# The residual behind the output projection: added by TensorE in PSUM instead of by VectorE

## The chip, the cores and the metric

One Trainium2 chip, one of its cores. The time is the device time of one execution in microseconds (us); lower is better. A time of a kernel is the median of its executions. The five engines run side by side, each with its instructions in a fixed order, and wait for each other by semaphores: TensorE (PE in the profile, its weight loads PEld), VectorE (DVE), ScalarE (ACT), GpSimd (POOL) and SyncE (SP), which here only issues transfers.

## The reference

A decoder layer in float32 on 64 sequences of 64 tokens with 128 channels, with three residual branches:

```
x = x + attn(layernorm(x))            # 16 heads of 8, q = k = v = x Wv + bv, then Wo and bo
x = x + xattn(layernorm(x), ctx, ctx) # 16 heads of 8, softmax, no projection
x = x + ffn(layernorm(x))             # SwiGLU: one shared expert and the best of 7 experts of each token
```

The change is at the end of the first line: the sum of x and the projected attention output, and the mean and variance of that sum, from which the query of the second line is made.

## The kernel before

The 4096 tokens are 32 units (U) of 128 tokens (two sequences). The first part of the program, `phase_a`, is a software pipeline written out step by step: in step t each engine works on several units at once, and the table `LAG` says which. Unit t is normalised and transposed, unit t-1 is projected (`proj`) and its self-attention scores are computed (`S_s`), unit t-2 gets its softmax and is weighed (`soft_s`), unit t-3 gets its output projection (`out`) and the bias (`xb`), unit t-4 its query and cross-attention scores and softmax (`q`), unit t-5 to t-7 the rest of cross attention. 32 units and lags up to 7 make 39 steps; TensorE and ScalarE leave the step form after step 33 and run a tail written out by hand. Nothing schedules: each engine's `body` is its order within a step.

Then come the router, the shared expert for the 32 units, the sorting of tokens by expert, and 38 tiles of expert rows. That part is about 170 us long and is not touched.

What happens to a unit around the change, in order: VectorE divides the weighed values by the sums of the softmax (`on_s`). SyncE writes them to a buffer in device memory and reads them back in another layout (`orow`), one step later. TensorE transposes `orow` (L619), ScalarE copies the result to `onT` (L890), TensorE multiplies `onT` by the output weights into a PSUM buffer (`ps_wo`, L624). GpSimd has in the meantime added the bias to the unit's rows of x (`p_xb`, L426). At the beginning of its next step VectorE adds `ps_wo` to these rows (L1120, tile `rows_all`), takes statistics of the sum (`st_s`, L1049) and makes mean and variance (`mv`, L1060). GpSimd subtracts the mean (`xn_s`, L409), TensorE transposes `xn_s` (`query`, L597), ScalarE copies it to `qT` (L884), and TensorE computes the cross scores (L545, tile `ring,qT`).

Names in the rows: L545 with `k_s,pT` are the self-attention scores, `mx_s` and `pr_s` the maxima over them and the differences, L842 the exponentials, L554 the transposes of the exponentials, L849 their copies out of PSUM (`prT`), L566 the weighing, L855 and L576 the copy and the transpose back (`oT`). The same with x in place of s is cross attention.

TensorE's order within a step is: `query`, projection of unit t-1 (L636, L643), `oT_x` back, cross scores, transposes of `pr_s`, weighing x and s, transposes of `xn_p` and `orow`, `oT_s` back, output projection (L624), self-attention scores (L545), transposes of `pr_x` (L554).

Of the kernel before, what the change touches and what calls it, by code (L numbers as in the profile page):

```python
# [29 lines left out]
U = B // NB  # L30
# [33 lines left out]
def build(nc, x, ctxk, ctxv, wv, bv, wo, bo, rw, rb, wup, wdn, ident, hmask, tri, small, tokens, out):  # L64
    ctx = ExitStack()
    with ctx:
# [307 lines left out]
        def _(pool):  # L374
# [27 lines left out]
            def body(t, u, live):  # L402
                i = t % 2
                pool.wait_ge(sem("mv_set"), 2)
                if live("q"):
                    pool.wait_ge(sem("s_mv"), at(u["q"]))
                    if u["q"] >= 1:
                        pool.wait_ge(sem("s_qT"), u["q"])
                    nc.gpsimd.tensor_scalar(xn["s"][:], x_all[:, u["q"], :], mv[i][:, 0, 0:1], None,  # L409
                                            ALU.subtract).then_inc(sem("s_xn"), 1)  # L410
# [118 lines left out]
        def _(pe):  # L529
# [91 lines left out]
            def project(u):  # L621

                pe.wait_ge(sem("s_onT"), at(u))
                nc.tensor.matmul(ps_wo, onT[:], wo_sb[:], start=True, stop=True).then_inc(sem("s_wo"), 1)  # L624

            def body(t, u, live):
                if t == LAG["q"]:
# [201 lines left out]
        def _(act):  # L829
# [56 lines left out]
            def output(u):  # L886
# [2 lines left out]
                    act.wait_ge(sem("s_wo"), u)  # L889
                nc.scalar.copy(onT[:], ps_oT).then_inc(sem("s_onT"), 1)  # L890

            def body(t, u, live):
                if live("pv_x"):
                    turned("x", u["pv_x"], 0)
# [46 lines left out]
                    nc.scalar.copy(kx_second, zero[:, 0:1].broadcast_to([P, CHUNK * NB * HG * S])).then_inc(sem("kx_zero1"), 1)  # L941
                if live("q"):
                    exp("x", t, u["q"], 1)

            phase_a(body, last=LAST_FULL)
            step = {u: u + LAG["q"] for u in (U - 2, U - 1)}
# [6 lines left out]
            output(U - 1)  # L953
            turned_rows(2)
            exp("x", step[U - 2], U - 2, 0)
            exp("x", step[U - 2], U - 2, 1)
            turned("x", U - 2, 0)
            query(U - 1)
# [76 lines left out]
        def _(dve):  # L1035
# [7 lines left out]

            nc.vector.memset(kx[:, 0:CHUNK // 2, :, :, :], 0.0).then_inc(sem("kx_zero0"), 1)

            def moments(k, u):
                if u >= 1:
                    dve.wait_ge(sem(f"{k}_mv"), u)
                nc.vector.bn_stats(st[k][:], x_all[:, u, :]).then_inc(sem(f"{k}_st"), 1)  # L1049

            def mean_variance(k, t, u):
                dve.wait_ge(sem(f"{k}_st"), at(u))
# [53 lines left out]
            def body(t, u, live):  # L1106
                if live("st_x"):
                    dve.wait_ge(sem("x_x"), at(u["st_x"]))
                    moments("x", u["st_x"])
                if live("norm"):  # L1110
                    if u["norm"] in X_LOADS:
                        dve.wait_ge(sem(X_LOADS[u["norm"]][0]), X_LOADS[u["norm"]][1])
                    moments("p", u["norm"])
                if live("out"):
                    invert("s", u["out"])
                    normalise("s", u["out"])
                if live("q"):
                    dve.wait_ge(sem("p_xb"), at(u["q"]))
                    dve.wait_ge(sem("s_wo"), at(u["q"]))
                    nc.vector.tensor_tensor(x_all[:, u["q"], :], ps_wo, x_all[:, u["q"], :], ALU.add).then_inc(sem("s_x"), 1)  # L1120
                if live("st_x"):
                    mean_variance("x", t, u["st_x"])
                if live("q"):
                    dve.wait_ge(sem("s_x"), at(u["q"]))
                    moments("s", u["q"])
                if live("norm"):
                    mean_variance("p", t, u["norm"])
                if live("q"):
                    mean_variance("s", t, u["q"])
                if live("soft_s"):  # L1130
                    maxima("s", u["soft_s"])
                    soften("s", u["soft_s"], 0)
                    soften("s", u["soft_s"], 1)
                if live("on_x"):
                    invert("x", u["on_x"])
                    normalise("x", u["on_x"])
                if live("q"):
                    maxima("x", u["q"])
                    soften_both("x", u["q"])
                if t == 1:  # L1140
                    nc.vector.memset(kx[:, CHUNK // 2:CHUNK, :, :, :], 0.0).then_inc(sem("kx_zero0"), 1)
                    dve.wait_ge(sem("l_first"), N_FIRST)
                    dve.wait_ge(sem("l_bv"), 16)
                    link(nc.vector.tensor_reduce(dmask[:], id_sb[:].rearrange("p (h d) -> p d h", d=DK), AX.X, ALU.add))
                    link(nc.vector.tensor_tensor(bvall_sb[:].rearrange("p (h d) -> p h d", d=DK),
                                                 bvall_sb[:].rearrange("p (h d) -> p h d", d=DK),
                                                 dmask[:, :].unsqueeze(1).broadcast_to([P, H, DK]), ALU.mult))
                    link(nc.vector.tensor_reduce(bvh[:], bvall_sb[:].rearrange("p (h d) -> p h d", d=DK), AX.X, ALU.add))
                    nc.vector.tensor_copy(bvrows_sb[:].rearrange("p (b h r) -> p b h r", b=NB, h=H),
                                          bvh[:, :].unsqueeze(1).unsqueeze(3).broadcast_to([P, NB, H, S // H])).then_inc(sem("bvrows"), 1)  # L1150
                if t == 2:
                    dve.wait_ge(sem("l_second"), N_SECOND)
                    dve.wait_ge(sem("bias"), 1)
                    nc.vector.tensor_tensor(obias[:], ps_bias, bo_sb[:], ALU.add).then_inc(sem("obias"), 1)
# [197 lines left out]
```

## Time and profile before

| | |
|---|---|
| median of 3 runs | 447.25 us (446.73 to 450.13) |
| span of the profiled execution | 447.9 us |
| steps of the pipeline shown in the rows below | about 34 us to 252 us of the span |
| granted TensorE clock, whole span | 0.985 |

The profile is of one execution, and its time is the span; what lies around the span is not in the numbers, and the span lies 0.65 us above the median of the runs. Rows of the timeline give the start and the duration of an instruction, or of a run of alike instructions, merged. Durations of neighbours on one engine can overlap, since an engine begins to read for the next instruction before the last has written; the distance from start to start says how long an instruction keeps its engine.

### The profile page before, as it was taken

To read this page: it belongs to the slowest core of one execution; us is meant where nothing else is said; L and a number is where in the kernel's file an instruction comes from. 1 tells how busy PE (TensorE), PEld (TensorE's weight loads), DVE (VectorE), ACT (ScalarE), POOL (GpSimd) and SP (SyncE) were. 2 spreads that over 40 slices of the span, in tenths; PEclk is the share of its full clock that TensorE was granted. 3 is DMA by queue.
4 is the path that set the end of the run, shared out by engine and by line. 5 is a ranking of instruction groups with operands and counts; after the bars stand their busy time and mean duration, and the time that the engine had idled before them with its cause. 6 is when DMAs were issued, how large, how long until landed. Compare 5 with 4: busy or idle time off the path is not lost. (4 is left out here: it accounts for less than half of the span.)

```text
span 447.9 us, 16458 instructions
## 1 busy us (share of the span) xinstructions
PE 420.6 (94%) x5570; PEld 314.2 (70%) x5571; DVE 312.5 (70%) x767; ACT 300.6 (67%) x685; POOL 300.5 (67%) x517
## 2 busy tenths in 40 slices
PE   7889999999999999999999999999999999999990
PEld 4545655555665655555565567899998899999990
DVE  5568999989999999999999854773333444545540
ACT  7858888788888888788888865432222465666650
POOL 8547768677877868687787655278888754444442
PEclk9999999999999999999999999899999999999995
DMA  6243444444444444453433379812222355530010
GB/s 108 37 83 46 77 52 56 69 53 80 57 80 65 70 74 60 88 64 63 46 57 39 32 131 198 268 44 71 77 80 76 85 129 137 137 105 25 27 35 0
DMA packets 181088, 34.51 MB, mean 77 GB/s; under 512 B 147347, under 2 KB 178582, under 8 KB 181024
## 3 DMA queue, kind: packets, MB, share of 16 engines
q1 hardware_dynamic: 170944, 23.63, 33.2%
q0 software_dynamic: 2864, 6.36, 4.1%
q10 hardware_dynamic: 7216, 3.69, 2.9%
q8 instruction: 37, 0.61, 0.6%
q14 instruction: 27, 0.22, 0.2%
HBM read 20.13 MB, written 15.74 MB: 80 GB/s over the span
## 5 line engine op out<-in xcount | busy, mean ns | idle before, releaser
L1162 DVE TENSOR_TENSOR gT<-gT,psum 128x384 f32<-128x384 f32 x66 | 36.6, 554 | 74.2 <-PE psum L744 51.8
L975 ACT ACTIVATE gT<-psum 128x384 f32<-128x384 f32 x70 | 34.1, 487 | 49.4 <-PE psum L744 36.0
L504 POOL DMA_INDIRECT out<-yrow,token x38 | 37.0, 973 | 40.7 <-DVE yrow L1281 26.5
L443 POOL TENSOR_TENSOR k_s<-pT,hmask_sb 128x1024 f32<-128x1024 f32 x32 | 60.9, 1903 | 2.1 <-ACT pT L904 2.0
L758 PE MATMUL psum<-wdn_sb,gT 128*128 (+1 forms) x420 | 59.9, 279 | 2.0 <-DVE yrow L1281 1.0
L409 POOL TENSOR_SCALAR xn_s<-rows_all,mv 128x128 f32<-128x128 f32 x32 | 19.4, 607 | 56.6 <-DVE mv L1060 37.7
L744 PE MATMUL psum<-fhT,wtile 128*128 128x128 f32 x456 | 57.2, 275 | 0.0
L758 PEld LDWEIGHTS psum<-wdn_sb,gT 128*128 128x128 f32 x420 | 52.4, 192 | 5.0 <-issue 3.9
L744 PEld LDWEIGHTS psum<-fhT,wtile 128*128 128x128 f32 x456 | 53.9, 192 | 0.1
L744 PE MATMUL psum<-hT_all,wup_sb 128*128 (+1 forms) x384 | 49.2, 280 | 0.0
L849 ACT COPY prT_x<-psum 128x512 f32<-128x512 f32 x64 | 34.6, 589 | 20.7 <-PE psum L554 20.4
L842 ACT ACTIVATE pr_x<-pr_x,rs 128x512 f32<-128x512 f32 x64 | 45.9, 723 | 1.4 <-DVE pr_x L1077 0.5
L744 PEld LDWEIGHTS psum<-hT_all,wup_sb 128*128 128x128 f32 x384 | 46.7, 197 | 0.0
L554 PEld LDWEIGHTS psum<-id_sb,pr_s 128*128 128x128 f32 x256 | 27.3, 141 | 26.7 <-ACT pr_s L842 26.6
L554 PEld LDWEIGHTS psum<-id_sb,pr_x 128*128 128x128 f32 x256 | 27.4, 141 | 24.8 <-ACT pr_x L842 24.8
L1070 DVE TENSOR_REDUCE mx_x<-psum 128x16 f32<-128x1024 f32 x32 | 39.2, 1225 | 7.8 <-PE psum L545 7.0
L1070 DVE TENSOR_REDUCE mx_s<-psum 128x16 f32<-128x1024 f32 x32 | 39.2, 1225 | 5.4 <-PE psum L545 4.3
L1085 DVE TENSOR_TENSOR pr_s<-psum,mx_s 128x512 f32<-128x512 f32 x64 | 41.2, 686 | 1.1
L1077 DVE TENSOR_TENSOR pr_x<-psum,mx_x 128x1024 f32<-128x1024 f32 x32 | 39.2, 1225 | 2.9
L842 ACT ACTIVATE pr_s<-pr_s 128x512 f32<-128x512 f32 x64 | 38.1, 627 | 1.7 <-DVE pr_s L1085 1.7
L554 PE MATMUL psum<-id_sb,pr_s 128*128 128x128 f32 x256 | 35.5, 280 | 0.8 <-ACT pr_s L842 0.7
L849 ACT COPY prT_s<-psum 128x512 f32<-128x512 f32 x64 | 34.5, 589 | 2.2
(150 smaller groups left out, 890.0 us busy)
## 6 DMA issues: line engine op xcount, KB each, us to landing
ring<-sorted_rows SPq DMA_DIRECT2D x30, 130.0 KB
sorted_rows<-nowhere_row SPq DMA_DIRECT2D x38, 65.0 KB, 2.3
wup_sb<-in_wup SPq DMA_DIRECT2D x7, 352.0 KB, 9.6
attention_out<-on_s SPq DMA_DIRECT2D x64, 32.0 KB, 2.9
ring<-in_ctxv SPq DMA_DIRECT2D x64, 32.0 KB, 3.3
orow<-attention_out SPq DMA_DIRECT2D x32, 64.0 KB
sorted_rows<-nowhere_row SPq DMA_DIRECT2D x3, 650.0 KB, 9.1
cross_keys<-in_ctxk ACTq DMA_DIRECT2D x14, 128.0 KB, 3.1
```

The source lines that it names most:

```text
L443: nc.gpsimd.tensor_tensor(k_s[:], pT[:].rearrange("p (b k) -> p b k", b=NB).unsqueeze(2).broadcast_to([P, NB, HG, S]), hmask_sb[:, 0:HG].u ...
L504: pool.indirect_dma_start(out=out, out_offset=bass.IndirectOffsetOnAxis(ap=token[p][:, 0:1], axis=0), in_=yrow[p][:, :], in_offset=None, b ...
L554: last = nc.tensor.transpose(ps_s[k][g][:, i * P:(i + 1) * P], pr[k][:, g, 2 * i:2 * i + 2, :].rearrange("p h k -> p (h k)"), id_sb[:])
L744: last = nc.tensor.matmul(ps[p][:, c * P:(c + 1) * P], weights[:, start:start + P], tokens, start=True, stop=True)
L758: last = nc.tensor.matmul(ps_y[p], gT[p][:, c, :], wdn_sb[:, expert, c, :], start=(c == 0), stop=(c == CH - 1))
L842: nc.scalar.activation(pr[k][:, g, :, :], pr[k][:, g, :, :], ACT.Exp, scale=rs[t % 2][:, 0:1] if k == "x" else float(DK) ** -0.5).then_inc ...
L849: nc.scalar.copy(prT[k][:, g, :, :].rearrange("p i q -> p (i q)"), ps_s[k][g]).then_inc(sem(f"{k}_prT"), 1)
L975: nc.scalar.activation(gT[p][:].rearrange("p c q -> p (c q)"), ps_gate[p][:, 0:CH * P], ACT.Silu).then_inc(sem("f_act"), 1)
L1070: nc.vector.tensor_reduce(mx[k][:], both(k), AX.X, ALU.max).then_inc(sem(f"{k}_mx"), G)
L1077: nc.vector.tensor_tensor(pr[k][:], both(k), mx[k][:].unsqueeze(3).broadcast_to([P, G, HG, S]), ALU.subtract).then_inc(sem(f"{k}_sub"), G)
L1085: nc.vector.tensor_tensor(pr[k][:, g, :, :], scores_of(k, g), mx[k][:, g, :].unsqueeze(2).broadcast_to([P, HG, S]), ALU.subtract).then_inc ...
L1162: nc.vector.tensor_tensor(g, g, ps_up[p][:, 0:CH * P], ALU.mult).then_inc(sem("f_g"), 1)
```

## The change

TensorE gets a second matmul behind the output projection, into the same PSUM buffer: the identity times the unit's rows of x. The sum with the residual then stands in PSUM. VectorE's addition is gone, and its statistics read PSUM. ScalarE copies the sum back to the rows of x, at the end of its step, behind the second exponential of cross attention; in the tail this copy stands between the two exponentials of unit 30. GpSimd's subtraction of the mean waits for that copy too.

```diff
@@ gpsimd, body @@
                     pool.wait_ge(sem("s_mv"), at(u["q"]))
+                    pool.wait_ge(sem("s_x"), at(u["q"]))
@@ tensor @@
             def project(u):
 
                 pe.wait_ge(sem("s_onT"), at(u))
-                nc.tensor.matmul(ps_wo, onT[:], wo_sb[:], start=True, stop=True).then_inc(sem("s_wo"), 1)
+                nc.tensor.matmul(ps_wo, onT[:], wo_sb[:], start=True, stop=False)
+                pe.wait_ge(sem("p_xb"), at(u))
+                nc.tensor.matmul(ps_wo, id_sb[:], x_all[:, u, :], start=False, stop=True).then_inc(sem("s_wo"), 1)
@@ scalar @@
+            def residual(u):
+                act.wait_ge(sem("s_wo"), at(u))
+                act.wait_ge(sem("s_st"), at(u))
+                nc.scalar.copy(x_all[:, u, :], ps_wo).then_inc(sem("s_x"), 1)
+
...
                 if live("q"):
                     exp("x", t, u["q"], 1)
+                if live("out"):
+                    residual(u["out"])
...
             exp("x", step[U - 2], U - 2, 0)
+            residual(U - 1)
             exp("x", step[U - 2], U - 2, 1)
@@ vector, body @@
-                if live("q"):
-                    dve.wait_ge(sem("p_xb"), at(u["q"]))
-                    dve.wait_ge(sem("s_wo"), at(u["q"]))
-                    nc.vector.tensor_tensor(x_all[:, u["q"], :], ps_wo, x_all[:, u["q"], :], ALU.add).then_inc(sem("s_x"), 1)
                 if live("st_x"):
                     mean_variance("x", t, u["st_x"])
                 if live("q"):
-                    dve.wait_ge(sem("s_x"), at(u["q"]))
-                    moments("s", u["q"])
+                    dve.wait_ge(sem("s_wo"), at(u["q"]))
+                    moments("s", u["q"], ps_wo)
```

TensorE in a step of the full pipeline, from the transpose back of self attention to the transposes of cross attention. Before:

```order
L576 MATMUL psum<-id_sb,oT_s 128x128 [waits s_oe]
L576 MATMUL psum<-id_sb,oT_s 128x128
L624 MATMUL psum<-wo_sb,onT 128x128 [waits s_onT]
L545 MATMUL psum<-k_s,pT 64x512 [waits s_prT,s_khd]
L545 MATMUL psum<-k_s,pT 64x512 x3
L554 MATMUL psum<-id_sb,pr_x 128x128 [waits x_exp]
```

After:

```order
L577 MATMUL psum<-id_sb,oT_s 128x128 [waits s_oe]
L577 MATMUL psum<-id_sb,oT_s 128x128
L625 MATMUL psum<-wo_sb,onT 128x128 [waits s_onT]
L627 MATMUL psum<-rows_all,id_sb 128x128 [waits p_xb]
L546 MATMUL psum<-k_s,pT 64x512 [waits s_prT,s_khd]
L546 MATMUL psum<-k_s,pT 64x512 x3
L555 MATMUL psum<-id_sb,pr_x 128x128 [waits x_exp]
```

One matmul has come in ahead of the self-attention scores. (The profile counts a float32 matmul of this kind as two, a transpose as one.)

VectorE at the beginning of a step, up to the maxima of self attention. Before:

```order
L1101 TENSOR_TENSOR on_s<-psum,rden_s 128x128 [waits s_out,s_rden]
L1120 TENSOR_TENSOR rows_all<-psum,rows_all 128x128 [waits s_wo,p_xb]
L1060 BN_AGGR mv<-st_x 128x2 [waits px_ve,px_mean,mv_set,x_st]
L1049 BN_STATS st_s<-rows_all 128x6 [waits s_mv,s_x]
L1060 BN_AGGR mv<-st_p 128x2 [waits px_ve,px_mean,mv_set,p_st]
L1060 BN_AGGR mv<-st_s 128x2 [waits s_ve,s_xn,mv_set,s_st]
L1070 TENSOR_REDUCE mx_s<-psum 128x16 [waits s_sc]
```

After:

```order
L1112 TENSOR_TENSOR on_s<-psum,rden_s 128x128 [waits s_out,s_rden]
L1071 BN_AGGR mv<-st_x 128x2 [waits px_ve,px_mean,mv_set,x_st]
L1060 BN_STATS st_s<-psum 128x6 [waits s_mv,s_wo]
L1071 BN_AGGR mv<-st_p 128x2 [waits px_ve,px_mean,mv_set,p_st]
L1071 BN_AGGR mv<-st_s 128x2 [waits s_ve,s_xn,mv_set,s_st]
L1081 TENSOR_REDUCE mx_s<-psum 128x16 [waits s_sc]
```

The addition is gone, and the statistics wait for the matmul (`s_wo`) where they waited for the addition (`s_x`).

ScalarE at the end of a step and the beginning of the next. Before:

```order
L842 ACTIVATE pr_x<-pr_x,rs 128x512 [waits s_rs,x_sub]
L849 COPY prT_x<-psum 128x512 [waits x_pv,x_turn] x2
L884 COPY qT<-psum 128x128 [waits x_sc,s_qT]
L904 ACTIVATE pT<-psum,bv_sb 128x128 [waits s_khd,s_sc,p_pv,p_p]
L842 ACTIVATE pr_s<-pr_s 128x512 [waits s_sub] x2
```

After:

```order
L845 ACTIVATE pr_x<-pr_x,rs 128x512 [waits s_rs,x_sub]
L898 COPY rows_all<-psum 128x128 [waits s_st,s_wo]
L852 COPY prT_x<-psum 128x512 [waits x_pv,x_turn] x2
L887 COPY qT<-psum 128x128 [waits x_sc,s_qT]
L912 ACTIVATE pT<-psum,bv_sb 128x128 [waits s_khd,s_sc,p_pv,p_p]
L845 ACTIVATE pr_s<-pr_s 128x512 [waits s_sub] x2
```

A copy has come in between the last exponential and the copies of the transposed cross-attention weights.

## Rows read from the trace of the kernel before

**Rows 1.** Busy time by stretch: us, PE, PEld, DVE, ACT, POOL, granted clock, DMA.

```profile
60.00:240.00 180.00, 176.14 (x2979) 105.94 (x2975) 165.58 (x370) 152.44 (x372) 138.26 (x254) 1.00 0.45 65
```

**Rows 2.** VectorE's maxima from 31 to 259 us: durations in ns, first and last start.

```profile
L1070 DVE TENSOR_REDUCE mx_s<-psum x29: 1223/1225/1226, 34.1 to 251.7; 128x16 f32<-128x1024 f32 x29
```

**Rows 3.** Who waited for whom, 60 to 240 us: us in total, times, longest.

```profile
POOL xn_s L409 <- DVE mv L1060: 30.7, 20, 1.9
...
DVE mx_x L1070 <- PE psum L545: 3.7, 16, 0.3
...
PEld psum L619 <- DMA orow<-attention_out: 1.9, 7, 0.5
...
DVE mv L1060 <- issue: 1.2, 4, 0.4
```

**Rows 4.** Timeline of a step: start us, us, engine, line, operation.

```profile
211.76 1.09 PE L545 MATMUL psum<-k_s,pT 64*64 64x512 f32 x8
...
212.12 0.72 ACT L842 ACTIVATE pr_x<-pr_x,rs 128x512 f32<-128x512 f32 x1
...
212.77 0.18 DVE L1060 BATCH_NORM_AGGREGATE mv<-st_s 128x2 f32<-128x6 f32 x1
...
212.99 1.23 DVE L1070 TENSOR_REDUCE mx_s<-psum 128x16 f32<-128x1024 f32 x1
213.12 0.61 POOL L409 TENSOR_SCALAR xn_s<-rows_all,mv 128x128 f32<-128x128 f32 x1 [1.41 <-DVE mv L1060]
213.47 1.07 ACT L849 COPY prT_x<-psum 128x512 f32<-128x512 f32 x2 [0.63 <-PE psum L554]
...
213.78 0.33 PE L597 MATMUL psum<-id_sb,xn_s 128*128 128x128 f32 x1
...
214.20 0.41 POOL L426 TENSOR_TENSOR rows_all<-rows_all,obias 128x128 f32<-128x128 f32 x1
...
214.25 1.29 DVE L1085 TENSOR_TENSOR pr_s<-psum,mx_s 128x512 f32<-128x512 f32 x2
...
215.02 1.18 ACT L842 ACTIVATE pr_s<-pr_s 128x512 f32<-128x512 f32 x2
...
217.18 0.59 ACT L849 COPY prT_s<-psum 128x512 f32<-128x512 f32 x1
...
218.75 0.44 PE L576 MATMUL psum<-id_sb,oT_s 128*128 128x128 f32 x2
...
219.02 0.44 PE L624 MATMUL psum<-wo_sb,onT 128*128 128x128 f32 x2
...
219.39 1.09 PE L545 MATMUL psum<-k_s,pT 64*64 64x512 f32 x8
219.51 0.29 DVE L1101 TENSOR_TENSOR on_s<-psum,rden_s 128x128 f32<-128x128 f32 x1
219.61 0.25 ACT L933 COPY xnT<-psum 128x128 f32<-128x128 f32 x1
219.72 0.28 DVE L1120 TENSOR_TENSOR rows_all<-psum,rows_all 128x128 f32<-128x128 f32 x1
...
219.92 0.17 DVE L1060 BATCH_NORM_AGGREGATE mv<-st_x 128x2 f32<-128x6 f32 x1
```

**Rows 5.** Timeline of TensorE in the expert part: passes back to back.

```profile
400.59 0.83 PE L758 MATMUL psum<-wdn_sb,gT 128*128 x6
401.26 0.27 PE L801 MATMUL psum<-id_sb,fx 128*128 128x128 f32 x1
```

**Rows 6.** Timeline of the tail: last projection, and the exponentials behind it.

```profile
263.91 0.14 PEld L619 LDWEIGHTS psum<-id_sb,orow 128*128 128x128 f32 x1 [0.31 <-DMA orow<-attention_out]
...
264.91 1.35 ACT L842 ACTIVATE pr_x<-pr_x,rs 128x512 f32<-128x512 f32 x2
```

**Rows 7.** Timeline of VectorE: the maxima at the two ends of the shortest period.

```profile
34.10 1.23 DVE L1070 TENSOR_REDUCE mx_s<-psum 128x16 f32<-128x1024 f32 x1
...
41.68 1.22 DVE L1070 TENSOR_REDUCE mx_s<-psum 128x16 f32<-128x1024 f32 x1
```

More of the change, by code:

```diff
@@ L1044, in _, with moments @@
             nc.vector.memset(kx[:, 0:CHUNK // 2, :, :, :], 0.0).then_inc(sem("kx_zero0"), 1)
-            def moments(k, u):
+            def moments(k, u, rows):
                 if u >= 1:
                     dve.wait_ge(sem(f"{k}_mv"), u)
-                nc.vector.bn_stats(st[k][:], x_all[:, u, :]).then_inc(sem(f"{k}_st"), 1)
+                nc.vector.bn_stats(st[k][:], rows).then_inc(sem(f"{k}_st"), 1)
             def mean_variance(k, t, u):
@@ L1108, in body @@
                     dve.wait_ge(sem("x_x"), at(u["st_x"]))
-                    moments("x", u["st_x"])
+                    moments("x", u["st_x"], x_all[:, u["st_x"], :])
                 if live("norm"):
@@ L1112, in body @@
                         dve.wait_ge(sem(X_LOADS[u["norm"]][0]), X_LOADS[u["norm"]][1])
-                    moments("p", u["norm"])
+                    moments("p", u["norm"], x_all[:, u["norm"], :])
                 if live("out"):
```

## The prediction

> **What bounds the kernel now.** I read the busy times by stretch first, then the timeline of one step, then the waits. In the pipeline's full steps VectorE is busy 165.58 of 180 us (92%) and TensorE 176.14 (98%) [rows 1]. Neither figure decides: TensorE's rows overlap, and VectorE's do too. So I looked for the round that closes on itself in each step. The maxima `mx_s` come 29 times between 34.1 and 251.7 us: 28 periods of 7.77 us on average [rows 2].
>
> The timeline shows the round [rows 4]. `mx_s` starts at 212.99, the differences `pr_s` at 214.25, their exponentials on ScalarE at 215.02, the second copy `prT_s` at 217.18; TensorE weighs, ScalarE copies `oT_s`, TensorE transposes it back at 218.75, runs the output projection at 219.02 and the scores of self attention at 219.39. These last 1.09, and the maxima follow 0.14 us behind their end (211.76 + 1.09 = 212.85, then 212.99). From 212.99 to 219.39 are 6.40 us, plus 1.09 and 0.14 makes 7.63. That is also the distance of the two scores in these rows (211.76 to 219.39): nothing in this round has slack, and the step lasts as long as the round. The output projection, where the change puts its matmul, is in it. VectorE's addition is not: it starts at 219.72, after the scores have started.
>
> Two things lengthen some steps from 7.63 to the mean of 7.77. `orow` comes back late from memory in 7 steps of 60 to 240 us, 1.9 us in total; and VectorE now and then loses some 0.3 us ahead of `mv` with nothing to wait for (1.2 us in 4) [rows 3], which looks like instructions being fetched.
>
> A second round runs through the query: `mv` at 212.77, `xn_s` on GpSimd 213.12 to 213.73, TensorE's query at 213.78 [rows 4]. TensorE arrives there at about the same time from the transposes before, so this round is nearly as long, but it also contains the projection and scores, through TensorE's order.
>
> **The added matmul.** It is a float32 matmul of 128 columns, as L624 is, two passes. What a pass costs in a chain: six passes of L758 take 400.59 to 401.26, 0.67 us, so 0.11 each, with different weights each time [rows 5]. The other end is L624 itself in the step, 0.37 us from its start to the scores for two passes [rows 4]; but that holds one start behind a wait for `onT` and one switch to the tiles of 64 of the scores, and both are there already. The new passes stand between the two, their weights are the identity, and their wait for `p_xb` is long over (GpSimd adds the bias at 214.20, five us earlier). I take 0.11 each, 0.22 us a step, and keep 0.37 a step as the upper end. All of it lies ahead of the scores, so all of it is in the round: 7.63 becomes 7.85.
>
> **The addition taken from VectorE.** It keeps VectorE from 219.72 to 219.92, 0.20 us a step [rows 4]. The maxima behind it wait for the scores, which are later now; so the gain becomes a wait of VectorE ahead of `mx_s`. Statistics from PSUM: the only rows of this shape that read PSUM are the addition itself (0.28) and `on_s` (0.29); I take no difference, and up to 0.1 us would be hidden in the same wait.
>
> **The copy on ScalarE.** A PSUM copy of this shape takes 0.25 (`xnT`) [rows 4]. ScalarE ends its second exponential at 212.84 and starts the next copy at 213.47, having waited 0.63 for TensorE's transposes. The copy fits in, and the wait grows by 0.22. Its own waits are early: the projection starts at 219.02 and would end at 219.46 + 0.22 = 219.68; the statistics follow `mv<-st_x`, which moves up to where the addition starts (219.72), and end by about 220.2. The exponential that is then running ends no earlier than 220.4 (212.84 and one period of 7.63). Behind it stand only copies that wait for TensorE anyway.
>
> **The new wait on GpSimd.** `xn_s` needs the copy: end of the exponential 212.84, copy to about 213.05, and GpSimd starts 0.17 behind a signal (`mv` ends 212.95, `xn_s` starts 213.12), so about 213.22. That is 0.10 later than now, but TensorE gets to the query 0.22 later than now. About 0.1 us of slack is left. Were the copy 0.2 us later than I think, GpSimd would set the query and cost 0.1 us a step.
>
> **The sum.** 28 periods of 7.85 are 219.8 us, against 217.6 now. Late `orow`s: each has 0.22 us more to arrive in, so of 1.9 us in 7 steps (2.3 for all 28) at least 2.3 - 9 x 0.22 = 0.3 remains; uneven ones leave more, I take 0.8. Fetch stalls: those on VectorE are covered where they fall now, but ScalarE and VectorE have a different number of instructions in a step, so their places drift into the round; I take 0.7 (two or three stalls). That makes 221.3, +3.7. Outside these periods lie four projections (steps 3, 4, 33 and the tail): 0.9, less 0.2 of the 0.31 that TensorE waits for the last `orow` in any case. In the tail ScalarE's copy stands between the two exponentials that start at 264.91, and TensorE's transposes of the second, the query behind them among them, wait for it [rows 6]: +0.3. In all +3.7 + 0.7 + 0.3 = +4.7. On the profiled execution of 447.9 that is a span of 452.6. The span lies 0.65 above the median of the runs, 447.25, so I forecast 452.0.
>
> **Rivals.**
> (a) *VectorE is the bound.* Its 92% speaks for it, and GpSimd waits 30.7 us for `mv` [rows 3]. Then the addition's 0.20 us is won in each of 32 steps and the matmul hides: 447.25 - 6.4 = 440.8. Against it: `mx_s` follows the scores by the 0.14 that it also takes elsewhere, and VectorE waits 3.7 us for the cross scores, 16 times [rows 3]; an engine that waits in most steps is not the bound. It decides from the point where VectorE's own work up to `mx_s` ends after the scores do, which it does only in the steps with a stall.
> The Trainium skill would lean this way: "Perfetto Trace Analysis", section "Identifying the Most-Contended Engine", says to judge TensorE by the share of its weight loads and not by that of its matmuls, and to relieve the most contended engine first. By that rule TensorE stands at 105.94 of 180 us (59%) [rows 1], VectorE at 92% is the one to relieve, and the time would be that of this rival. The timeline speaks against the rule here, since the round passes through several engines in turn.
> (b) *The passes are dear*, 0.37 a step because the wait for `p_xb` or the change of source breaks TensorE's run of loads. Then a step is 8.00, 28 are 224.0, late `orow`s vanish, stalls 0.7: +7.1, with 1.4 outside and 0.3 in the tail +8.8, 456.0.
> (c) *The query becomes the bound.* The copy's signal comes 0.2 us later than worked out, and each step costs 0.1 more: 28 x 0.1 on top of the forecast, 454.8.
> (d) *It does little*: the steps that have a stall or a late `orow` swallow the matmul's 0.22 wholly, and the fetch stalls end up under waits. 28 x 7.80 (the shortest period now, 34.10 to 41.68 or 7.58, plus 0.22) [rows 7] is 218.4, with 0.3 for late `orow`s +1.1, with 0.7 outside +1.8: 449.0.
>
> **Chances.** Forecast 0.50, (a) 0.04, (b) 0.12, (c) 0.14, (d) 0.20. The likeliest's own range is 450.3 to 453.5. Over all, from just under (d) to just over (b): 448.7 to 456.5, which leaves out (a) and some 0.1 at the two ends. A measurement of this kernel can tell about 1% from no change, 4.5 us; the forecast lies just above that line at 451.7. Of the forecast's share a little over half is above, with (b) and (c) all: slower 0.52; (d) and the rest of the forecast: same 0.44; faster 0.04.
>
> **What the changed profile would show.** Right: `mx_s` comes every 7.85 us or so with less spread than now; L627 starts 0.11 behind L625's second pass and the scores 0.6 us behind L625's start; VectorE busy falls by some 0.2 us a step while its wait ahead of `mx_s` appears among the waits; the waits for `orow` shrink; ScalarE's copy starts right behind the exponential and `prT_x` still waits for TensorE. Wrong: TensorE waits at the query for `xn_s` (then (c)); the scores 0.7 us or more behind L625 (then (b)); periods at or under 7.63 (then (a)). What could make the prediction wrong beyond these is where the fetch stalls fall, which I can't work out from the rows.

## The result, and the profile after

The changed kernel takes 453.75 us (median; 452.46 to 455.12), beside 447.46 for the kernel before in the same comparison: a ratio of 1.0133, with an interval of 1.009 to 1.0177. It is slower by 6.3 us. The profiled execution took 452.46, of which 450.7 is its span.

The same views as before the prediction, now of the changed kernel. First the busy times from 60 to 240 us (columns as in [rows 1]):

```profile
60.00:240.00 180.00, 175.68 (x2976) 107.53 (x2974) 157.25 (x341) 151.72 (x387) 135.79 (x248) 1.00 0.44 64
```

VectorE has become 8.3 us freer in these 180 us (157.25 after 165.58), and the kernel is slower. That is worth remembering when the next table of busy shares is read.

VectorE's maxima over the full steps, the row that answers to [rows 2]:

```profile
L1081 DVE TENSOR_REDUCE mx_s<-psum x29: 1224/1225/1226, 34.0 to 257.1; 128x16 f32<-128x1024 f32 x29
```

The 28 periods take 223.1 us (217.6 before), 7.97 each. The waits from 60 to 240 us (as [rows 3]):

```profile
POOL xn_s L410 <- ACT rows_all L898: 35.6, 21, 2.5
...
DVE mx_s L1081 <- PE psum L546: 10.9, 21, 0.8
...
PEld psum L620 <- DMA orow<-attention_out: 2.7, 6, 0.9
...
DVE mv L1071 <- issue: 0.3, 1, 0.3
...
PEld psum L598 <- POOL xn_s L410: 0.2, 1, 0.2
```

What VectorE saved stands in the second row: it now waits for the scores of self attention in 21 steps. GpSimd waits for ScalarE's copy, as the change makes it, but TensorE hardly ever waits for GpSimd (last row): that wait is hidden. `orow`, however, is waited for longer than before (2.7 after 1.9), though each step gives it more time.

One undisturbed step in the timeline (as [rows 4]):

```profile
129.18 0.73 ACT L845 ACTIVATE pr_x<-pr_x,rs 128x512 f32<-128x512 f32 x1
129.21 1.09 PE L546 MATMUL psum<-k_s,pT 64*64 64x512 f32 x8
...
129.81 0.26 ACT L898 COPY rows_all<-psum 128x128 f32<-128x128 f32 x1
...
130.32 0.61 POOL L410 TENSOR_SCALAR xn_s<-rows_all,mv 128x128 f32<-128x128 f32 x1 [1.59 <-ACT rows_all L898]
130.44 1.23 DVE L1081 TENSOR_REDUCE mx_s<-psum 128x16 f32<-128x1024 f32 x1 [0.48 <-PE psum L546]
130.79 1.38 SPq L174 DMA_DIRECT2D ring<-in_ctxv  x2
...
130.92 1.07 ACT L852 COPY prT_x<-psum 128x512 f32<-128x512 f32 x2 [0.86 <-PE psum L555]
131.05 0.14 PEld L598 LDWEIGHTS psum<-id_sb,xn_s 128*128 128x128 f32 x1
...
132.74 0.73 SPq L174 DMA_DIRECT2D orow<-attention_out  x1
...
136.42 0.44 PE L625 MATMUL psum<-wo_sb,onT 128*128 128x128 f32 x2
...
136.70 0.39 PE L627 MATMUL psum<-rows_all,id_sb 128*128 128x128 f32 x2
...
137.01 1.09 PE L546 MATMUL psum<-k_s,pT 64*64 64x512 f32 x8
...
138.24 1.23 DVE L1081 TENSOR_REDUCE mx_s<-psum 128x16 f32<-128x1024 f32 x1
```

From 130.44 to 138.24 is 7.80, the usual length: 17 of the 28 periods are 7.80 to 7.83. The scores start 0.59 behind L625 where before they started 0.37 behind L624 [rows 4]: the added matmul costs 0.22. ScalarE's copy starts at 129.81 as the exponential ends, and still 0.86 is left in which ScalarE waits for the transposes.

Now a step that something did happen to:

```profile
231.53 1.33 SPq L174 DMA_DIRECT2D attention_out<-on_s  x2
...
232.54 1.23 DVE L1081 TENSOR_REDUCE mx_s<-psum 128x16 f32<-128x1024 f32 x1 [0.48 <-PE psum L546]
232.90 2.81 SPq L174 DMA_DIRECT2D ring<-in_ctxv  x2
...
236.75 0.33 SPq L174 DMA_DIRECT2D orow<-attention_out  x1
...
238.64 0.14 PEld L620 LDWEIGHTS psum<-id_sb,orow 128*128 128x128 f32 x1 [0.82 <-DMA orow<-attention_out]
```

SyncE spends 2.81 us on two issues that took 1.38 above, issues `orow` 3.85 behind their start, where it was 1.95 behind, and TensorE waits 0.82. This is the late `orow` of the prediction: it is late because its issue is. But the long issue is not the whole reason. It ends at 235.71, and SyncE then still waits until 236.75, for `attention_out` to land; it waits for that landing in every step (13.7 us in 23 between 60 and 240 us). The issue of `attention_out` took 1.33 here and in the undisturbed step (where it started at 129.42). From its start to the issue of `orow` are 3.32 us there and 5.22 here, so the landing came 1.9 later, more than the 1.4 that the long issue took. Whether the long issue held the landing up or both have one cause, the rows don't say.

### The profile page after: what moved, and what is told of

Read it like the earlier page. It is cut to its first block and busy times, and to the rows that moved or that the text cites. A ratio compares the mean times of both kernels' runs of the same rounds, so it can differ in the third digit from the quotient of the medians.

```text
span 450.7 us, 16617 instructions
## 1 busy us (share of the span) xinstructions
PE 422.6 (94%) x5634; PEld 319.6 (71%) x5635; DVE 304.7 (68%) x735; ACT 304.1 (67%) x717; POOL 300.5 (67%) x517
## 5 line engine op out<-in xcount | busy, mean ns | idle before, releaser
L761 PE MATMUL psum<-wdn_sb,gT 128*128 (+1 forms) x420 | 58.4, 275 | 1.2 <-DVE yrow L1288 0.6
L845 ACT ACTIVATE pr_s<-pr_s 128x512 f32<-128x512 f32 x64 | 39.2, 630 | 1.7 <-DVE pr_s L1096 1.7
L546 PE MATMUL psum<-ring,qT 64*64 64x512 f32 x256 | 34.8, 614 | 1.5 <-ACT qT L887 1.1
```

The source lines that it names most:

```text
L546: last = nc.tensor.matmul(ps_s[k][g][S * b:S * (b + 1), :], q[S * g:S * (g + 1), S * b:S * (b + 1)], keys[S * g:S * (g + 1), b, :, :].rear ...
L761: last = nc.tensor.matmul(ps_y[p], gT[p][:, c, :], wdn_sb[:, expert, c, :], start=(c == 0), stop=(c == CH - 1))
L845: nc.scalar.activation(pr[k][:, g, :, :], pr[k][:, g, :, :], ACT.Exp, scale=rs[t % 2][:, 0:1] if k == "x" else float(DK) ** -0.5).then_inc ...
```

## The experiments

"28 periods" are from the first to the last of the 29 `mx_s`; "undisturbed" is the distance of two `mx_s` in the short steps, those without a late `orow` and without another stall (two figures where the steps without a late `orow` are of two kinds); the last two columns are TensorE's weight loads waiting between 60 and 240 us. Ratios are to the kernel before, run on the same chip in the same session; chips differ by some us (the kernel before took 446.4 to 450.6), so medians of different groups are not to be compared.

```
kernel                   median   ratio (interval)         28 periods  undisturbed  orow  xn_s
group 1 (before 448.78)
  matmul_alone           457.49   1.0206 (1.0172-1.0239)   223.6       7.81         1.7   2.2
  no_matmul              451.88   1.0077 (1.0047-1.0107)   219.3       7.60, 7.78   2.4   4.4
  two_matmuls            459.49   1.0257 (1.0223-1.0291)   226.5       8.03         1.1   -
  matmul_early           452.26   1.0102 (1.0067-1.0136)   220.9       7.60, 7.78   3.5   4.0
group 2 (before 446.44)
  before_values_later    469.53   1.0500 (1.0462-1.0538)   238.7       7.6          13.2  2.1
  after_values_later     465.63   1.0386 (1.0346-1.0426)   237.9       7.81         9.5   0.2
  early_values_later     465.28   1.0385 (1.0334-1.0436)   237.7       7.6          14.0  2.1
  early_free_query       469.23   1.0444 (1.0401-1.0487)   241.5       7.58         15.7  -
second profiles (before 446.64)
  a_again                450.18                            220.6       7.81         1.3   0.2
  b_again                445.91                            217.5       7.64         1.5   2.6
group 3 (before 450.63)
  early_free             458.24   1.0147 (1.0100-1.0195)   222.0       7.58         6.7   0.3
  before_one_value_later 452.57   1.0031 (0.9999-1.0062)   223.0       7.64         5.8   2.6
```

Averaged over all steps of the 28 periods in which TensorE does not wait for `orow`, a period is 7.71 us in both profiles of the kernel before and 7.83 in both of the changed one; 7.90 in `matmul_alone`, 7.74 in `no_matmul`, 7.73 in `matmul_early`, 7.65 in `early_free`.

**Only the matmul.** TensorE multiplies the rows into a piece of PSUM that nobody reads, and VectorE adds as before (TensorE's lines, against the changed kernel):

```
-  matmul(ps_wo, onT, wo_sb, start=True, stop=False)
+  matmul(ps_wo, onT, wo_sb, start=True, stop=True)
   pe.wait_ge(sem("p_xb"), at(u))
-  matmul(ps_wo, id_sb, x_all[:, u, :], start=False, stop=True)
+  matmul(ps_dup, id_sb, x_all[:, u, :], start=True, stop=True)
```

> The kernel before with only TensorE's added matmul, at the same place, behind the wait for the bias; its result goes to a PSUM region that nobody reads, and VectorE still adds the residual and ScalarE copies nothing. Theory (the matmul lies in the round that sets the step): the shortest periods of mx_s go from 7.63 to 7.81 or a little over (7.63 + 0.22 at most), and the time is at least that of the changed kernel: about +6 us on before, 453 to 455. Rival (the cost comes from the copy on ScalarE and the new wait on GpSimd): 447 to 449, periods at 7.63.

The undisturbed step is 7.81 again, as the theory had it, and the 28 periods are 223.6. The matmul by itself makes the whole lengthening of the undisturbed step; taking the addition from VectorE gives nothing back in it. The median, 457.49, is above the 453 to 455 expected, and this kernel is even slower than the changed one. In part that is what the changed kernel hides: here VectorE still stalls ahead of `mv` (1.4 us in 5 waits between 60 and 240 us, 0.3 in 1 in the changed kernel). Such a step lasts 7.91 or more, and in the one behind it TensorE waits for `xn_s` (2.2 us in 6, there 0.2 in 1) and the step lasts 7.97; the sixth of these follows a stall ahead of `st_s`. So the average step without a late `orow` is 7.90, not 7.83. Its expert part, which no edit touches, is 4.0 us longer in the one profile (167.1 and 163.1), and why, I can't say.

**All but the matmul.**

```
-  matmul(ps_wo, onT, wo_sb, start=True, stop=False)
   pe.wait_ge(sem("p_xb"), at(u))
-  matmul(ps_wo, id_sb, x_all[:, u, :], start=False, stop=True)
+  matmul(ps_wo, onT, wo_sb, start=True, stop=True)
```

> The changed kernel without the second matmul: the residual behind self attention is left out of the sum; the statistics from PSUM, the copy on ScalarE and the waits stay. Theory: everything but the matmul is free or a small gain, since the addition is gone from VectorE: shortest periods 7.58 to 7.63, time 444 to 448. Rival (copy and wait cost): 449 or more, with TensorE waiting for xn_s at the query.

The theory missed; the rival had it. Without the matmul the rest of the change is not faster than the kernel before but 0.8% slower. (That total holds more than the step: the router sees other rows here, and in the profile the first of the 29 `mx_s` comes 3.5 us later, behind a late `orow` of 1.7 us at 25.0.) The timeline shows what it costs in the step:

```profile
123.53 0.18 DVE L1070 BATCH_NORM_AGGREGATE mv<-st_s 128x2 f32<-128x6 f32 x1
123.73 0.25 ACT L897 COPY rows_all<-psum 128x128 f32<-128x128 f32 x1
...
124.24 0.61 POOL L410 TENSOR_SCALAR xn_s<-rows_all,mv 128x128 f32<-128x128 f32 x1 [1.55 <-ACT rows_all L897]
124.90 0.14 PEld L598 LDWEIGHTS psum<-id_sb,xn_s 128*128 128x128 f32 x1 [0.28 <-POOL xn_s L410]
```

The statistics are ready at 123.71, the copy at 123.98 (it stands behind the second exponential), GpSimd starts 0.26 behind it, and TensorE waits 0.28 for `xn_s` at the query. That happens in 16 waits between 60 and 240 us, 4.4 us in all; in the kernel before there were 6, of 2.5 us. Of the 21 steps without a late `orow`, those in which TensorE waits for `xn_s` last 7.77 or more in all but two of 13, and the 8 others 7.56 to 7.71. So the copy has a price of its own in about half of the steps, which the matmul's 0.22 hides in the changed kernel.

**The matmul twice.** The second adds a tile that is in SBUF anyway.

```
-  matmul(ps_wo, id_sb, x_all[:, u, :], start=False, stop=True)
+  matmul(ps_wo, id_sb, x_all[:, u, :], start=False, stop=False)
+  matmul(ps_wo, id_sb, nowhere_row[:, 0:D], start=False, stop=True)
```

> The changed kernel with a third matmul behind the two, the identity times a tile of zeros, two more passes at the same place. Theory: every step 0.22 us longer again, shortest periods 7.81 to 8.03, time +5 to +7 us on the changed kernel if late orows don't change, less if the longer step gives them time (then +3 to +5). Rival (one wait broke TensorE's run and the passes themselves are nearly free): less than +2.

```profile
152.80 0.44 PE L625 MATMUL psum<-wo_sb,onT 128*128 128x128 f32 x2
...
153.08 0.39 PE L627 MATMUL psum<-rows_all,id_sb 128*128 128x128 f32 x2
...
153.30 0.39 PE L628 MATMUL psum<-nowhere_row,id_sb 128*128 128x128 f32 x2
...
153.62 1.09 PE L546 MATMUL psum<-k_s,pT 64*64 64x512 f32 x8
```

L628 starts 0.22 behind L627, the scores 0.82 behind L625 (0.59 in the changed kernel), and the step goes from 7.81 to 8.03. A third data point on one line: 7.6, 7.81, 8.03. The 28 periods grow by only 3.4 us, not by 28 x 0.22 = 6.2, because `orow` is late in two steps only. That the longer step hid the others is likely but not shown: the second profile of the changed kernel, below, has three late ones without it, and its 28 periods are 6.0 shorter than these.

**The matmul ahead of the projection**, where TensorE waits for `onT` (the transpose of `orow` then needs another place in PSUM):

```
   turn_output(u["out"])
+  residual_first(u["out"])      # matmul(ps_wo, id_sb, x_all[:, u, :], start=True, stop=False)
   turn_back("s", u["soft_s"])
   ...
-  matmul(ps_wo, onT, wo_sb, start=True, stop=False)
-  pe.wait_ge(sem("p_xb"), at(u))
-  matmul(ps_wo, id_sb, x_all[:, u, :], start=False, stop=True)
+  matmul(ps_wo, onT, wo_sb, start=False, stop=True)
```

> The changed kernel with the residual's matmul put first: it opens the sum in PSUM right behind the transpose of orow, where TensorE waits for the copy oT_s, and the output projection adds to it; the transpose of orow goes to another bank, so that nothing comes between the two. The last unit keeps the order of the changed kernel. Theory: the matmul falls into TensorE's gap ahead of the transpose back of self attention (0.29 us from start to start in fast steps) and costs nothing, and the gain on VectorE remains: shortest periods 7.58 to 7.62, time 445 to 448. Rival (TensorE has no room there, or the sums' wait for the bias or the extra wait delays orow): periods at 7.8, 452 to 455.

It missed. The shortest steps are the 7.58 to 7.62 of the theory, so TensorE had room for the matmul. But many steps last 7.78:

```profile
121.03 1.23 DVE L1093 TENSOR_REDUCE mx_s<-psum 128x16 f32<-128x1024 f32 x1 [0.26 <-PE psum L547]
...
128.57 0.25 ACT L910 COPY rows_all<-psum 128x128 f32<-128x128 f32 x1
128.81 1.23 DVE L1093 TENSOR_REDUCE mx_s<-psum 128x16 f32<-128x1024 f32 x1 [0.26 <-PE psum L547]
...
129.74 0.14 PEld L599 LDWEIGHTS psum<-id_sb,xn_s 128*128 128x128 f32 x1 [0.28 <-POOL xn_s L411]
```

The matmul is out of the round, and in about half of the steps without a late `orow` (9 of 17) TensorE waits for `xn_s`, and the second round sets the length: second exponential, copy, `xn_s`, query, cross scores, exponentials. The average of these 17 is 7.73, where the changed kernel has 7.83: of the matmul's 0.22 about 0.1 is won back.

**The values behind `orow`.** To take the late `orow` away, SyncE issues the cross values after it, in the kernel before, in the changed one, and in the one with the early matmul:

```
   load(o_dram <- on_s)                  # two issues, as before
-  cross_values(t - 3)                   # ring<-in_ctxv, two issues
   sp.wait_ge(sem("s_out"), ...)         # attention_out has landed
   load(orow <- o_rows)
+  cross_values(t - 3)
```

> The kernel before with one move on SyncE alone: in each step the transfers of the cross attention's values (ring from in_ctxv) are issued behind those of the self attention's rows (orow from attention_out), not ahead of them. Theory (about once a step one issue on SyncE lasts 1.0 to 2.8 us; where it falls ahead of the rows' issue, TensorE waits for orow): the issue of orow gets some 1.3 us of time in hand, TensorE's weight load waits for orow no more than 0.1 us in all between 60 and 240 us, the 28 periods of mx_s come to 213.5 to 215.5 us instead of 217.56, and the median falls by 2 to 4 us, to 444 to 446. Rival (the late rows are late on the DMA engines, not at their issue): the waits for orow stay at 2 us or more, and the median at 447 to 449.

> The changed kernel with the same move on SyncE. Theory: its steps without a late orow last 7.81 us, so 28 of them come to 218.7 to 219.5 us instead of 223.1, and the median to 449 to 450.5, which is 4 to 5.5 us above the kernel before with the same move: 0.2 us for each of 28 steps (5.6) less some stalls. Rival (the change itself, not the place of a slow issue, makes orow late): periods stay at 222 us or more and the median at 453 to 454.

> The same move, and the added matmul issued ahead of the projection (start of the sum instead of its end), so that it lies in TensorE's wait for onT. Theory: no waits for orow are left, but the query's round (ScalarE's copy behind the second exponential, GpSimd's subtraction, TensorE) bounds the step at 7.7 to 7.79: 28 periods of 216 to 218 us, and a median of 446.5 to 448.5. Rival (the late orow was all that kept the early matmul from being free): steps of 7.58 to 7.64, 28 of them 213 to 214.5 us, and 444 to 445.5.

All three missed by far: about 4 to 5% slower, with more waits for `orow`, not fewer. SyncE's own waits from 60 to 240 us, first with this order in the kernel before, then in the kernel before as it is (second profile):

```profile
SPq L174 <- DMA attention_out<-on_s: 45.4, 21, 3.4
...
SPq L174 <- DVE on_s L1101: 0.8, 2, 0.5
```

```profile
SPq L174 <- DVE on_s L1101: 24.2, 20, 1.9
SPq L174 <- DMA attention_out<-on_s: 14.9, 24, 1.0
```

The values used to fill the time in which `attention_out` lands. Behind `orow` they come on top of it, and SyncE has no time left in which it waits for `on_s`: it has become the bound. One of its steps:

```profile
69.69 1.32 SPq L174 DMA_DIRECT2D attention_out<-on_s  x2
...
74.43 0.35 SPq L174 DMA_DIRECT2D orow<-attention_out  x1
74.82 1.36 SPq L174 DMA_DIRECT2D ring<-in_ctxv  x2
76.23 1.77 SPq L174 DMA_DIRECT2D ring<-cross_keys  x4
...
78.04 0.36 SPq L174 DMA_DIRECT2D sorted_rows<-nowhere_row  x1
...
78.72 1.32 SPq L174 DMA_DIRECT2D attention_out<-on_s  x2
```

Issues of 1.32, 0.35, 1.36, 1.77 and 0.36 are 5.16 us, and the landing from 71.01 to 74.43 is 3.42: 8.6 of the 9.03 us of this step. `attention_out`'s landing varies, and on average over 21 steps is waited for 2.2.

With this order the changed kernel is not 4 to 5.5 us slower than the kernel before, as expected, but faster: 465.63 and 469.53, and the intervals of their ratios do not overlap. Its 28 periods are 0.8 shorter. Where SyncE is the bound, the matmul's 0.22 a step no longer shows.

**The query freed of the copy.** ScalarE copies into a tile of its own, and GpSimd reads the rows without waiting. It ran on top of the early matmul, with the values later and, since SyncE was then in the way, again without:

```
-  pool.wait_ge(sem("s_x"), at(u["q"]))
-  nc.scalar.copy(x_all[:, u, :], ps_wo)
+  nc.scalar.copy(x_aside[:], ps_wo)
+  pe.wait_ge(sem("s_x"), at(u))         # ahead of the query's transpose, which reuses ps_wo
```

> As the kernel with the early matmul and the values later, but ScalarE copies the sum to a tile of its own, and GpSimd's subtraction no longer waits for the copy: it reads the rows without self attention's part. Left out: self attention's part of the residual in everything behind the copy, so the router sees other rows and the expert part's time may differ. It has the same instructions on each engine. Theory (the query's round through the copy bounds the steps of 7.77 to 7.79): TensorE's waits for xn_s fall from some 4 us to under 1 between 60 and 240 us, and the periods go to 7.58 to 7.64 (28 of them 213 to 214.5 us). Rival (it is ScalarE's own load, not the wait for its copy): the periods stay at 7.7 to 7.79.

> The kernel with the early matmul, SyncE's order as in the kernel before, and again a copy to a tile of its own that GpSimd's subtraction doesn't wait for. Left out: self attention's part of the residual in everything behind the copy, so the expert part's time may differ. SyncE's order is no longer in the way, so this tells what the earlier run with that order could not. Theory (the query's round through the copy gives the steps of 7.77 to 7.80): those steps are gone, undisturbed ones last 7.56 to 7.64, TensorE waits for xn_s under 1 us between 60 and 240 us (4.0 in the early matmul's run), and the 28 periods come to 216 to 218.5 us instead of 220.94. Rival (ScalarE is too full with the copy): steps of 7.7 to 7.8 stay and the 28 periods come to 220 or more.

```profile
121.79 0.18 DVE L1084 BATCH_NORM_AGGREGATE mv<-st_s 128x2 f32<-128x6 f32 x1
121.82 0.26 ACT L911 COPY x_aside<-psum 128x128 f32<-128x128 f32 x1
122.13 0.61 POOL L411 TENSOR_SCALAR xn_s<-rows_all,mv 128x128 f32<-128x128 f32 x1 [1.35 <-DVE mv L1084]
122.23 1.23 DVE L1094 TENSOR_REDUCE mx_s<-psum 128x16 f32<-128x1024 f32 x1 [0.26 <-PE psum L547]
122.84 0.14 PEld L600 LDWEIGHTS psum<-id_sb,xn_s 128*128 128x128 f32 x1
...
129.81 1.23 DVE L1094 TENSOR_REDUCE mx_s<-psum 128x16 f32<-128x1024 f32 x1 [0.26 <-PE psum L547]
```

With the values later the total missed (28 periods of 241.5, expected 213 to 214.5), because TensorE waited 15.7 us for `orow`; of waits for `xn_s` none was left, as the theory said. The rows are of the run without that move. The same instructions on each engine, only GpSimd's wait is for `mv`: 122.23 to 129.81 is 7.58, and TensorE's waits for `xn_s` fall from 4.0 to 0.3 us. The theory of the second round holds: the wait for the copy made the 7.78, not ScalarE's load. The total missed (222.0, expected 216 to 218.5), because `orow` was late in 11 waits, 6.7 us; SyncE's wait for the landing was 18.7 us in this run (14.9 above). One of them:

```profile
190.82 1.33 SPq L176 DMA_DIRECT2D attention_out<-on_s  x2
192.20 1.39 SPq L176 DMA_DIRECT2D ring<-in_ctxv  x2
195.65 0.33 SPq L176 DMA_DIRECT2D orow<-attention_out  x1
...
198.12 0.14 PEld L624 LDWEIGHTS psum<-id_sb,orow 128*128 128x128 f32 x1 [1.22 <-DMA orow<-attention_out]
```

Both pairs of issues have their usual lengths, and yet `orow` is issued 4.83 behind the start of `attention_out` (3.32 in the undisturbed step above): the landing alone is late. So a long issue is not needed for a late `orow`.

**One value behind `orow`**, one ahead, in the kernel before.

> The kernel before with one of the two issues of the cross values on SyncE behind the issue of orow, and one still ahead. With both behind, SyncE itself became the bound: its issues took 122.4 us of 180 (5.8 per step), it waited 45.4 us for attention_out to land (2.15 per step), with some 0.4 of gaps 8.4, as long as the steps got (8.5). Theory: with one behind, that sum is 5.8 + 1.3 + 0.4 = 7.5, under the step of 7.64 but with only 0.1 to 0.2 left (0.85 now), so an issue that lasts 1 us longer delays the next on_s instead of orow: 28 periods of 216.5 to 219 us, and a median within 1.5 us of the kernel before. Rival (the time in hand ahead of orow is what counts): orow is late in at most two steps, the 28 periods fall to 214.5 to 216, and the median by 1.5 to 3 us, a version faster than both.

No gain: the ratio is 1.0031 (0.9999 to 1.0062). The landing is waited for 32.2 us and `on_s` 9.6; `orow` is late in 5 waits that cost 5.8 us, the longest 2.2. The median is 1.9 us above that of the kernel before, just outside the 1.5 of the theory (by the ratio it is 1.4), and the 223.0 of this profile's periods are well above the expected 216.5 to 219. None of the orders tried beats the kernel before, and neither does any other version here.

**Both kernels profiled again.**

> The changed kernel once more, for a second profile. If the late orows come from where a slow issue on SyncE falls, which is not the kernel's doing, their places among the steps differ between the two profiles while steps without one stay at 7.80 to 7.81; the 28 periods lie between 219.5 and 224 us. If they belong to the change, the same steps are late again.

> The kernel before once more, for a second profile. Its 28 periods of mx_s lie between 215.5 and 218.5 us with steps of 7.58 to 7.65 where orow is not late; and if the expert part of the first profile was slow by chance, it takes 163 to 165 us instead of 166.4.

```profile
L1081 DVE TENSOR_REDUCE mx_s<-psum x29: 1223/1225/1225, 33.9 to 254.5; 128x16 f32<-128x1024 f32 x29
...
PEld psum L620 <- DMA orow<-attention_out: 1.3, 3, 0.8
```

The changed kernel's second profile has the same undisturbed step of 7.80 to 7.81, but its 28 periods take 220.6, 2.5 us less, and its waits for `orow` are half as long (1.3 after 2.7). Some of the same steps are late in both, others in one only, so neither half of the expectation holds alone. The kernel before repeats its 217.5, and its expert part takes 162.5 where the first profile had 166.4: that profile was 4 us unlucky there.

## Why the prediction came out as it did

The forecast was 452.0, +4.7 on the kernel before; measured were 453.75 and +6.3, just above the likeliest case's own range (450.3 to 453.5) and inside the whole one. The direction and the main mechanism were right. That the number came so near is in part luck: the step's term was 1.1 us too large, and the term for late `orow`s and stalls 2.9 too small in one profile and 0.4 in the other. The single executions of the second profiles differ by only 4.3 (450.18 and 445.91).

*The round and the added matmul.* Right. 0.11 a pass, 0.22 a step, all of it in the round: shown by the rows L625 to L546, by `matmul_alone` (7.81 with VectorE's addition still there) and by `two_matmuls` (8.03). The predicted step was 7.85 and is 7.81: the undisturbed step of the kernel before varied between 7.58 and 7.65, and I added to 7.63. The shortest one, 7.58, plus 0.22 is the 7.80 of the timeline. I had said that the round of 7.63 has no slack; the extra 0.05 may be a touch of the query's round (no run tests it), since VectorE waited for the cross scores 16 times in the kernel before [rows 3] and does so twice in the changed one (0.7 us). This term was 28 x 0.04 = 1.1 us too large.

*The addition on VectorE.* Right that it gives nothing in the round: it returned as VectorE's wait ahead of `mx_s`, 10.9 us in 21. What it gave is cover for VectorE's stalls (7.90 in `matmul_alone`, 7.83 in the changed kernel). Rival (a) falls, by its own sign (periods at or under 7.63): VectorE's busy time fell by 5%, and the periods are 7.81. The Trainium skill's page "Perfetto Trace Analysis", section "Identifying the Most-Contended Engine", would have had VectorE relieved first; on this kernel the measurement decides against that.

*The copy on ScalarE.* Right for the changed kernel: it stands in a wait that was 0.63 and is now 0.86.

*The wait on GpSimd.* Right that some 0.1 us of slack is left: the copy ends at 130.07, `xn_s` 130.93, and TensorE loads it at 131.05, with a wait in one step only, so rival (c) falls. (GpSimd starts 0.25 behind the end of the copy, where I took 0.17.) But I treated this slack as safe, whereas it exists only under the matmul: without the matmul in the round, `no_matmul` and `matmul_early` have steps of 7.78 beside those of 7.6, and `early_free` shows that it is the wait for the copy that makes them. The change thus has two costs one above the other, at 7.81 in every step and at 7.78 in about half, and the larger hides the smaller. Removing the matmul's cost alone wins 0.1 a step, not 0.22.

The query's round touched the kernel before too, which the prediction left out where it named two things that lengthen steps. The waits of its first profile have, between 60 and 240 us:

```profile
PEld psum L597 <- POOL xn_s L409: 2.5, 6, 0.5
```

Five of these six steps follow one in which VectorE stalled, four times ahead of `mv` and once ahead of `st_s`; the four of the six without a late `orow` last 7.75. So a stall of VectorE lengthened two steps there. In the changed kernel one such wait is left (0.2).

*Late `orow`s and stalls: the mis-sized term.* I put 0.8 + 0.7 = 1.5 us above the undisturbed steps. Measured: 223.1 - 28 x 7.81 = 4.4 in one profile, 220.6 - 218.7 = 1.9 in the other. Split by steps, the `orow`s are the part that was off: 4.0 us in 8 steps and 1.3 in 3, for the 0.8. The rest is 0.4 and 0.6, for the 0.7: VectorE's stalls did go under its wait (`mv` 0.3 us, once). That the rest is instruction fetches, as the prediction calls it, no run shows.

The mistake was to take the delays of one profile of the kernel before, subtract 0.22 from each and add a small margin. A longer step does give each `orow` that much more, but the delays are drawn anew in each profile, and those of 0.8 to 0.9 (three in one profile, one in the other) are too long for 0.22 to matter. In most late steps what comes late is the landing of `attention_out`, behind which SyncE issues `orow` (in one of the eight, that from 201.1, `orow` is issued at its usual place and is slow itself). In the first profile of the changed kernel seven of the eight late steps have an issue of `attention_out` or of the values that lasts 1.15 to 2.1 us instead of 0.61 to 0.68, but five steps with such an issue have no late `orow`; in `early_free` five of 15 late steps have none. Whether the long issues are a cause or a companion of the late landings is open.

*Outside the periods* I had 0.7 + 0.3 = 1.0. The expert part's first matmul starts at 287.61 and 286.28 in the two profiles of the changed kernel, and at 281.47 and 281.64 in those of the kernel before. That is 6.1 and 4.6 later (predicted 4.7), of which 5.5 and 3.1 are in the periods; so 0.6 and 1.5 lie outside, around the 1.0. The whole difference lies ahead of the expert part, whose times (163.1 and 162.1; 166.4 and 162.5) show none of the change. The medians' 6.3 is near the worse of the two pairs; what part of it is the `orow`s of an average execution, two profiles can't say.

*The rivals.* (b), the dear passes, falls: 0.22, not 0.37. (d) falls by its time, 449.0, but not in all of its parts: its step was 7.80, and most of the stalls did end up under waits (what is above the undisturbed steps without the late `orow`s was 1.6 us in the kernel before and is 0.4 and 0.6 here). What it had wrong is that the late `orow`s all but vanish.

What stays open: what makes `attention_out` land late, and what makes an issue on SyncE last longer. The Trainium skill, "Perfetto Trace Analysis", section "DMA Instruction — HWDGE (DVE, Sync)", counts the wait for the shared descriptor generator and the writing of the descriptors into such an issue's span. No run here shows which of them grew, or whether it is something else. Open too are the 4.0 us of `matmul_alone`'s expert part.

## What to carry to other kernels

Where a pipelined step is a closed round through several engines, an operation costs what it adds to the round, whatever the busy shares say: work taken from an engine at 92% gave nothing in the undisturbed step, and 0.22 us on TensorE came through in full. Before trusting a slack, ask which round is next, by how much and in how many steps (here 0.03 us below the first, in about half of them): it tells what undoing the first cost would win. And count the queue that issues the DMAs among the engines, with its waits for data to land: reordering two issues on it cost more than three times what the change did, and the change's own cost vanished behind it.

## What was unexpected of the hardware

- One issue on SyncE has very different lengths: two of `ring<-in_ctxv` took 1.38 us in most steps and 2.81 in one. Such long ones come in series, and their place drifts through the step: in the seven steps from 49.6 to 107 us of the changed kernel's first profile, one issue of `attention_out` or of the values lasted 1.15 to 1.72 us in each, where 0.61 to 0.68 is usual.
- The landing of `attention_out` in memory can be late by 1.5 us though its own issue and the one behind it have their usual lengths: in `early_free` SyncE issued `orow` 4.83 us behind the start of `attention_out`, and 3.32 in an undisturbed step.
- SyncE's wait for that landing was 14.9 us in 24 with the values ahead and 45.4 in 21 with them behind. Of the 1.5 us more per wait, 1.4 is the issue of the values, which no longer fills it.
- Statistics read from PSUM cost what those from SBUF do, within 0.02 us (`st_s` 0.28 from PSUM in the changed kernel, where `st_x` and `st_p` from SBUF take 0.28 too; from SBUF `st_s` itself took 0.30).
- The expert part, whose code is the same in all these kernels, took 162.1 to 167.1 us between profiles (without the three kernels that change what the router sees), nearly as much as the effect under study. Only the split at its first matmul makes single profiles comparable.
